# A graph layer and a routed expert layer on one core: the adjacency read through GpSimd's queue with the cast in the transfer

## What is computed

```
deg = max((adj != 0).sum(-1), 1)
# layer 1, on n = layernorm(x)
a_norm = rsqrt(deg) * (adj + eye) * rsqrt(deg)
x = x + relu((a_norm @ n + n) @ W + b)
# layer 2, on xf = layernorm(x)
probs = softmax(xf @ Wr + br);  top 2, weights divided by their sum
y = sum over experts e of combine[:, e] * (gelu(xf @ W1[e] + b1[e]) @ W2[e] + b2[e])
x = x + xf + y
```

## Time and profile before

| | us |
|---|---|
| median of 3 runs | 747.54 (747.32 to 748.49) |
| the profiled execution, its own time | 748.18 |
| the profiled execution, its span | 746.5 |
| mean granted TensorE clock | 0.951 of full speed |

### The profile page before, as it was taken

How to read it: one execution, slowest core, us unless ns; L and a number is a source line. 1 busy time by engine, 2 the same in 40 slices (tenths; PEclk the granted TensorE clock), 3 DMA queues, 4 the chain that set the end, 5 groups by cost and what they waited for, 6 DMA issues and landing times.

```text
span 746.5 us, 17744 instructions
## 1 busy us (share of the span) xinstructions
PE 603.4 (81%) x4798; PEld 462.1 (62%) x4799; DVE 472.2 (63%) x1366; ACT 344.5 (46%) x568; POOL 316.9 (42%) x296
## 2 busy tenths in 40 slices
PE   0049988887888989888887258999999999999994
PEld 0038866776666767677666225666666777777773
DVE  4966776676666767667666525766666565655562
ACT  2746656556464665655654113434343223322331
POOL 3631434344343443533425572454443444444444
PEclk9999999999999999999999558999999999999998
DMA  9548999999999999999984434565674444344320
GB/s 295 186 141 223 268 238 246 240 240 234 235 236 236 239 247 239 235 239 248 241 205 145 183 124 107 114 157 123 130 167 72 76 77 82 61 68 77 66 53 0
DMA packets 65915, 126.76 MB, mean 170 GB/s; under 512 B 9547, under 2 KB 40559, under 8 KB 65360
## 3 DMA queue, kind: packets, MB, share of 16 engines
q1 hardware_dynamic: 40240, 72.27, 37.8%
q10 hardware_dynamic: 10368, 35.66, 19.1%
q0 software_dynamic: 15264, 18.31, 13.9%
HBM read 103.71 MB, written 25.83 MB: 174 GB/s over the span
## 4 chain that ended last, share of the span: by engine, by line
DMA 39%; PE 26%; issue 13%; POOL 9%; DVE 6%; ACT 4%; POOLq 1%; ACTq 1%; SPq 1%; DVEq 0%
DMA rows<-feat,posi 23%; DMA out_dram<-orows,at_xg 9%; PE bank L536 9%; PE bank L559 8%; DMA abuf<-in_adj_dram 4%; POOL rows L1219 3%; PE bank L544 3%; ACT feat L635 2%; DMA wall<-in_x_dram 2%; PE bank L516 2%; POOL orows L1202 2%; POOL rows L1237 2%; PE bank L479 1%; PE bank L481 1%; DVE wall L826 1%
## 5 line engine op out<-in xcount | busy, mean ns | idle before, releaser
L479 PE MATMUL bank<-wall,at_xg 128*128 128x257 f16 x1024 | 244.7, 280 | 0.0
L481 PE MATMUL bank<-wall,at_xg 128*128 128x256 f16 x1024 | 244.4, 279 | 0.0
L1252 POOL DMA_INDIRECT out_dram<-orows,at_xg x79 | 127.5, 1614 | 164.5 <-DMA out_dram<-orows,at_xg 105.0
L601 ACT ACTIVATE a<-abuf 128x1024 f16<-128x1024 f32 x128 | 134.7, 1052 | 93.1 <-DMA abuf<-in_adj_dram 61.6
L744 ACT ACTIVATE a<-a 128x512 f32<-128x512 f32 x79 | 49.8, 630 | 184.7 <-DVE a L1072 184.7
L536 PE MATMUL bank<-wall,feat 128*128 x474 | 118.6, 387 | 10.3 <-issue 8.6
L479 PEld LDWEIGHTS bank<-wall,at_xg 128*128 128x128 f16 x1024 | 105.7, 103 | 14.7
L1078 DVE SCALAR_TENSOR_TENSOR wg<-bank,xseT 128x512 f16<-128x512 f32 x79 | 54.6, 692 | 92.1 <-ACT xseT L750 92.1
L1206 POOL TENSOR_TENSOR feat<-xf,feat 128x512 f16<-128x512 f32 x32 | 37.0, 1156 | 178.4 <-ACT feat L635 178.4
L816 DVE STREAM_TRANSPOSE at_xg<-a 128x512 int32<-128x512 int32 x128 | 90.6, 709 | 34.1 <-ACT a L601 24.7
L481 PEld LDWEIGHTS bank<-wall,at_xg 128*128 128x128 f16 x1024 | 102.5, 100 | 14.7
(11 more groups left out here) (152 smaller groups left out, 796.8 us busy)
## 6 DMA issues: line engine op xcount, KB each, us to landing
abuf<-in_adj_dram SPq DMA_DIRECT2D x64, 512.0 KB, 8.8
abuf<-in_adj_dram ACTq DMA_DIRECT2D x64, 512.0 KB, 12.3
wst<-in_L_ffn_W_dram SPq DMA_DIRECT2D x32, 512.0 KB, 5.3
at_xg<-rows SPq DMA_DIRECT2D x79, 136.0 KB, 2.4
out_dram<-orows SPq DMA_DIRECT2D x32, 128.0 KB
abuf<-in_L_ffn_b_dram SPq DMA_DIRECT2D x4, 1024.0 KB, 10.1
wall<-in_x_dram SPq DMA_DIRECT2D x8, 256.0 KB, 12.9
wall<-in_x_dram ACTq DMA_DIRECT2D x8, 256.0 KB, 13.2
```

The costliest lines, as they stand in the source:

```text
L479: both = [lambda: pe.matmul(ps_acc[odd][:, 0:D + 1], w, xh[:, j, 0:D + 1], start=j == 0, stop=j == T - 1), lambda: pe.matmul(ps_acc[odd][: ...
L481: lambda: pe.matmul(ps_acc[odd][:, 0:D], w, xl[:, j, :], start=False, stop=False)]
L601: act.activation(a16[:, c % 2, :].rearrange("p (a w) -> p a w", a=Q), arrived[:, k % 2, :, c * w:(c + 1) * w], ACT.Copy).then_inc(ev("cast ...
L1252: L.indirect_dma_start(out, bass.IndirectOffsetOnAxis(ap=info[r][:, 0:1].bitcast(U32), axis=0), orow[r], None, bounds_check=N - 1, oob_is_ ...
```

## The change

The adjacency's four DMAs per tile are issued by POOL, all four, and their destination is float16: `abuf` now holds four tiles of float16 in the bytes in which it held two of float32 (`AB = 4`), with one semaphore each. `cast`, its semaphore and `a16` are gone; DVE transposes straight out of `abuf`, and waits there for the tile's DMAs. SP and ACT issue no adjacency DMAs. The first three tiles are issued in POOL's prologue, between its steps on x; from then on POOL's step t begins with the four DMAs of tile t+3 (`more_adj`), ahead of `rstd1`; they wait until all chunks of tile t-1, which lay in the same buffer, are transposed.

The base is made by ACT alone: base = x1 * (rstd/2048 + 1) - mean * rstd/2048, with the two factors per token made by two small DVE instructions in front of `norm_x1` (`bs`). POOL's `make_base` is gone. At the very end of the phase `pads_before`, which lies in `xf`, waits for the last `low_part`.

The diff, cut:

```diff
 JC = CW // P
-CAST = 3
+AB = 4
 DEPTH = 3
...
 
-    abuf = sb("abuf", [P, 2 * Q * CW], F32)
-    arrived = abuf[:, :].rearrange("p (k a w) -> p k a w", k=2, a=Q)
-    b1all = abuf[:, :]
-    a16 = sb("a16", [P, 2, CW], F16)
+    abuf = sb("abuf", [P, AB * Q * CW], F16)
+    arrived = abuf[:, :].rearrange("p (k a w) -> p k a w", k=AB, a=Q)
+    b1all = abuf[:, :].bitcast(F32)
+    hgs = sb("hgs", [P, 2, H], F32)
     at_xg = sb("at_xg", [P, 2 * U * RW], F16)
...
     wst = sb("wst", [P, 2, DC * H], F32)
-    hg = [a16[:, k, :].bitcast(F32) for k in range(2)]
+    hg = [hgs[:, k, :] for k in range(2)]
     feat = sb("feat", [P, 2, TOPK, RW], F32)
...
     vr = sb("vr", [P, 2], F32)
+    bs = sb("bs", [P, 2], F32)
     lg = sb("lg", [P, E], F32)
...
     x_in = [sem(f"x_in{c}") for c in range(XC)]
-    a_in = [sem(f"a_in{k}") for k in range(2)]
+    a_in = [sem(f"a_in{k}") for k in range(AB)]
     w_in = [sem(f"w_in{k}") for k in range(2)]
...
 
-        eng.dma_start(arrived[b * PQ:(b + 1) * PQ, k % 2, :, :],
+        eng.dma_start(arrived[b * PQ:(b + 1) * PQ, k % AB, :, :],
                       adj_v[bass.ds(pair(i, k), 1), k % 2, b, :, :, :].rearrange("n i a c -> i (n a) c"))\
-           .then_inc(a_in[k % 2], 16)
+           .then_inc(a_in[k % AB], 16)
 
...
                 load_x(sp, c, b)
-            if c in (0, 2):
-                for b in QUEUE[0]:
-                    load_adj(sp, 0, c // 2, b)
         for dst, src in consts[0:2]:
...
         def load_b1():
-            sp.wait_ge(ev("cast"), T * CH)
+            sp.wait_ge(ev("at_made"), T * CH)
             b1_v = b1.rearrange("(c e) h -> c (e h)", c=CH).unsqueeze(1)
...
                 store_base(i, k - 3)
-            if is_(t, lambda t: t + 2 < T):
-                sp.wait_ge(ev("cast"), t * CH + CH)
-                for b in QUEUE[0]:
-                    load_adj(sp, i, k + 2, b)
             if isinstance(t, int) and t == T:
...
     def _(act):
-        def cast(i, k, c):
-
-            n = tile(i, k) * CH + c
-            act.wait_ge(a_in[k % 2], pair(i, k) * 16 * Q + 16 * Q)
-            if is_(n, lambda n: n >= 2):
-                act.wait_ge(ev("at_made"), n - 1)
-            w = CW // CH
-            act.activation(a16[:, c % 2, :].rearrange("p (a w) -> p a w", a=Q),
-                           arrived[:, k % 2, :, c * w:(c + 1) * w], ACT.Copy).then_inc(ev("cast"), 1)
-
         def cut_high_weights(i, which):
...
                 act.wait_ge(ev("b2_in"), 16)
-            act.activation(base[k % 2], xf[:, :], ACT.Copy, scale=1.0 / SX).then_inc(ev("base_scaled"), 1)
+            after(act, "base_scale", r)
+            after(act, "base_shift", r)
+            act.activation(base[k % 2], x1, ACT.Identity, scale=bs[:, 0:1], bias=bs[:, 1:2]).then_inc(ev("base_made"), 1)
 
...
                 load_x(act, c, b)
-            if c in (0, 2):
-                for b in QUEUE[1]:
-                    load_adj(act, 0, c // 2, b)
 
-        def more_adj(i, k):
-            act.wait_ge(ev("cast"), tile(i, k) * CH - CH)
-            for b in QUEUE[1]:
-                load_adj(act, i, k, b)
-
-        cast(0, 0, 0)
-        scale_x(0)
-        cast(0, 0, 1)
-        scale_x(1)
-        cast(0, 0, 2)
-        scale_x(2)
-        cast(0, 0, 3)
-        more_adj(0, 2)
-        scale_x(3)
+        for c in range(XC):
+            scale_x(c)
 
...
             for g in range(G):
-                if g % 2 == 0:
-                    k2, c2 = chunk(k, g // 2, CAST)
-                    if is_(tile(i, k2), lambda t2: t2 < T and (t2, c2) != (0, 3)):
-                        cast(i, k2, c2)
                 if g == 1 and has_v:
                     exps(v)
-                if g == 1 and is_(t, lambda t: 1 <= t < T - 2):
-                    more_adj(i, k + 2)
                 if g == 3 and has_s:
...
             n = tile(i, k) * CH + c
-            after(V, "cast", n)
+            V.wait_ge(a_in[k % AB], (tile(i, k) - k % AB) * (16 * Q // AB) + 16 * Q)
             if is_(n, lambda n: n >= CH):
...
             V.transpose(at[:, c, :].bitcast(I32).rearrange("p (n a i) -> p a n i", a=Q, i=PQ),
-                        a16[:, c % 2, :].bitcast(I32).rearrange("p (a n q) -> p a n q", a=Q, q=PQ))\
+                        arrived[:, k % AB, :, c * CW // CH:(c + 1) * CW // CH].bitcast(I32)
+                        .rearrange("p a (n q) -> p a n q", q=PQ))\
              .then_inc(ev("at_made"), 1)
...
                 after(V, "low_made", s - 1)
-                after(V, "base_scaled", s - 1)
+                after(V, "base_made", s - 1)
+            V.tensor_scalar(bs[:, 0:1], vr[:, 1:2], 1.0 / SX, 1.0, ALU.mult, ALU.add).then_inc(ev("base_scale"), 1)
+            V.tensor_scalar(bs[:, 1:2], mv[:, 0:1], vr[:, 1:2], -1.0 / SX, ALU.mult, ALU.mult).then_inc(ev("base_shift"), 1)
             V.tensor_scalar(xf[:, :], x1, mv[:, 0:1], vr[:, 1:2], ALU.subtract, ALU.mult)\
...
         after(V, "table_T", 0)
+        after(V, "low_made", T - 1)
         V.tensor_scalar(pads_before, ps_R[0:1, 2 * P:3 * P], 16.0, None, ALU.max).then_inc(ev("pads_table"), 1)
...
 
+        for b in range(Q):
+            load_adj(L, 0, 0, b)
         rstd0(0)
         rstd0(1)
+        for b in range(Q):
+            load_adj(L, 0, 1, b)
         low0(0)
...
         L.dma_start(rows[E * CAP:PLACES, :], pad[:, :]).then_inc(ev("padded"), 16)
+        for b in range(Q):
+            load_adj(L, 0, 2, b)
         low0(2)
...
 
+        def more_adj(i, k):
+            t = tile(i, k)
+            if is_(t, lambda t: t >= AB):
+                L.wait_ge(ev("at_made"), t * CH - (AB - 1) * CH)
+            for b in range(Q):
+                load_adj(L, i, k, b)
+
         def rstd1(s):
...
 
-        def make_base(i, k):
-            after(L, "base_scaled", tile(i, k))
-            L.tensor_tensor(base[k % 2], base[k % 2], x1, ALU.add).then_inc(ev("base_made"), 1)
-
         def low_part(s, odd):
...
             r, v = t - 2, t - 3
+            if is_(t, lambda t: t + AB - 1 < T):
+                more_adj(i, k + AB - 1)
             if is_(r, lambda r: 0 <= r < T):
...
                 low_part(r, odd)
-                make_base(i, k - 2)
             if is_(v, lambda v: 0 <= v < T):
```

## The result

The changed kernel takes 706.55 us, the median of 4 runs (704.46 to 707.11), against 747.85 (747.32 to 748.49, 4 runs) for the kernel before. The ratio is 0.944, with a 95% interval of 0.942 to 0.946. That is 5.6% less; 739 was forecast, inside a range of 695 to 795. The sign and the range held, the size did not: the gain is 41 us where 9 were forecast. The profiled execution took 704.46 us, its span 702.5.

A forecast was written before the change was run, and what follows sets the result against it. The prediction took POOL's serial step, P = 6.17 + 1.24 + 4I = 11.2 us with I = 0.95, as the new bound. Time = 748.2 + 4 + 26P + 16.3 - 321.2 = 738.5, forecast as 739 us, range 695 to 795.

The forecast's parts named there:

- the rival of cheap issues: POOL's DMA issues take 0.32 to 0.89 us, so PE may become the bound: 691 to 733 us, chance 0.24.
- the chain over POOL: POOL's serial step, from four issues to two row writes, becomes the new bound at 11.2 us: 733 to 747 us, chance 0.33.
- A loop over POOL and the row writes just as long: Kernel before: high_part, POOL's row writes and their landing (7.4 us) form a loop as long as the transfers.
- the transfer's rate: Adjacency loads with the cast in flight: 9 to 10 us a tile likely for all traffic, against 11.8 before.
- slow casts: Rival: the cast in flight lowers the transfers' rate, above 12.5 us a tile: 775 us and up, chance 0.15.
- unchanged transfers: Rival: transfers stay at 14.7 GB/s per engine, P = 11.8 us: 748 to 757 us, chance 0.10.
- dearer issues: Rival: each POOL issue costs more, from 1.05 us, delaying xf, high_part and low_part: 750 to 802 us, chance 0.16.
- the term I: POOL's time to issue one adjacency DMA, four a step ahead of its power: taken as 0.95 us.
- The front: Start of POOL's step, four issues with their gaps ahead of the power: 4 x 0.95 + 4 x 0.31, 5.0 us.
- P: Length of POOL's step in the graph phase, 6.17 + 1.24 + 4I: 11.2 us, counted for 26 steps.
- The rest of the chain: POOL's step without the issues and their gaps: power, DVE's factors and xf, high_part to first write, two writes: 6.17 us.
- The prologue: Before the steps: tile 0 lands near 20 to 22 us, delaying DVE's statistics; PE's first matmul 4 us later, bounds 0 and 9.

The follow-up runs named there:

- four powers: The changed kernel with four more small POOL power instructions in every step, between the four DMA issues and POOL's own power: 742.93 us, ratio 0.993.
- with two: The changed kernel with two more small POOL power instructions in every step, between the four DMA issues and POOL's own power: 718.87 us, ratio 0.960.
- the prologue's two edits: The changed kernel with DVE transposing tile 0's first chunk after x's statistics and POOL issuing tile 2 after its second low0: 698.09 us, ratio 0.931.

## Why the prediction was right in its parts and wrong in its size

The sign and the range held, the range because it took in the rival of cheap issues. The new bound that the prediction named, the chain over POOL, is not the bound of the changed kernel; PE is, with short waits for DVE.

**Right: the bound before.** Full queues were the bound, shown by the halved bytes (696). "A loop over POOL and the row writes just as long" was too much: shortened alone it gave 3 us, and with half the bytes its waits went.

**Right: what the casts on ACT are worth.** Nothing by themselves: with all of them in place, and half the bytes, a step takes 9.66 us.

**Right: the transfer's rate.** I took 19.6 GB/s per engine from the first tiles with x, measured is 20. That the two agree is in part luck: the 19.6 were float32 loads into both halves of the partitions at once, and nothing in that row told what a cast would do. The whole of the traffic then needed less than the 9.6 us forecast: share 0.86 of 9.79 us is 8.4 us a step. The rivals with slow casts or unchanged transfers are out, and so is that of dearer issues: the slowest of the 128 took 0.778 us.

**Right: the waits that go.** Those for the adjacency and for the rows' landing are gone from the profile, and the two-buffer run shows that the first needs loads issued further ahead than one step, as the deeper buffers allow.

**Wrong: the term I, POOL's time for an issue, and the gap beside it.** The step that failed was "For I the nearest row is POOL's one plain DMA, ... 0.895 us" with "I take I = 0.95" and "four issues with a gap of 0.31". Measured: 0.57 a piece back to back, 0.589 as a mean, no gap. The front is 2.3 us where 5.0 was in the sum. Two choices made this. The first: the one instance was POOL's first DMA of the program. In the changed kernel the same write of pad comes after eight others:

```profile
L1156 POOL DMA_DIRECT2D rows<-pad x1: 631/631/631, 42.5 to 42.5; - x1
...
L248 POOL DMA_DIRECT2D abuf<-in_adj_dram x128: 542/577/778, 6.5 to 327.7; - x128
```

The pad's write took 0.895 in the earlier trace rows and takes 0.631 here, and the slowest of the 128 loads, 0.778, is again the first. The second choice: the surcharge and the gap were read from the indirect writes, which are another kind of instruction. They still show both (1.07 us and 0.30 to 1.31 idle before); the plain loads show neither. The rows were few, and I treated the one instance as the middle of a range from 0.32 to 1.56 instead of a likely high value.

**What the other terms did.** With I at 0.57 and no gap the prediction's own sum gives P = 6.17 + 2.28 = 8.45 us, under PE's 9.3, that is its rival "issues are cheap, PE is the bound", at 691 us. The measured 704.5 differs from it by three things: step 3 comes 7.1 us later, not 4 (+3.1); the 28 steps take 273.5 us and not 260.4 (+13.1); the time after them is 3.4 shorter. The middle one is 0.5 us a step: PE's own work is 9.33 us, just what was said, and the 0.46 of idle time are nearly all waits for DVE (L416, 8.1 us in 24 steps, and L409, 2.7 in 5, together 0.45 a step). The five waits at L409, about 0.55 each, come with the return of the loop: every fourth step takes 10.3 us, the others 9.6. DVE is the busiest engine behind PE, at 84%. Its stall beside low_part is part of the 84; what the stall costs a step was not isolated.

**The rest of the chain came out 0.8 us long, and one gap in it had been hidden.** In the round with four powers above, all but the front takes 11.26 - 4.31 = 6.95 us, where the sum had 6.17. The two writes were 0.33 shorter (2.48 for 2.81). From the start of high_part to the first write it takes 3.17 us in the changed kernel (202.25 to 205.42), where 2.71 - 0.73 = 1.98 was said. After low_part POOL stands idle for 1.31 us before its first write. What it waits for is DVE. The write needs places and weights that DVE makes in a few small instructions; now they fall beside low_part, the conversion among them stalls until low_part ends, and the last of them ends at 204.39. The write begins 1.03 us later, and so it is in 23 of the 24 tiles between 100 and 340 us (the other took 1.36). In the kernel with only the base moved, DVE had ended 1.6 us or more before the write in 17 of 20 tiles, and there the gap was 0.17 us. So the 0.73 us of make_base do come out of the chain where DVE is early. In the changed kernel DVE is late, and they do not. With 6.95, which is taken from the run with four powers, the sum gives 6.95 + 3.33 = 10.3 with two (measured 10.32), and 6.95 + 2.28 = 9.2 for the changed kernel, which is the slack of about 0.55 us under its 9.79.

**The prologue.** Forecast: PE's first product 4 us later, bounds 0 and 9; measured 6.4. The mechanism was the one named. Tile 0 landed at 21.31, forecast 20 to 22, and the statistics of x's second chunk began at 21.95 instead of 16.02:

```profile
21.31 0.71 DVE L781 STREAM_TRANSPOSE at_xg<-abuf 128x512 int32<-128x512 int32 x1 [10.46 <-DMA abuf<-in_adj_dram]
```

Those 5.9 us alone, for which 4 had been put in, explain most of the size. The rest is where POOL's two low0 fall beside DVE. The first holds a small instruction of the third chunk's statistics for 4.66 us where it was 3.40. The second stood beside `scale_some` before, and stands beside DVE's low_x now. The six instructions of `scale_some`, before and after, then low_x and the low0 beside it:

```profile
35.10 5.94 DVE L826 TENSOR_SCALAR wall<-wall,mean,rstd 128x256 f32<-128x256 f32 x6 [0.27 <-POOL rstd L1166]
```
```profile
42.23 2.03 DVE L792 TENSOR_SCALAR wall<-wall,mean,rstd 128x256 f32<-128x256 f32 x6 [0.27 <-POOL rstd L1135]
...
47.00 5.40 DVE L768 TENSOR_TENSOR wall<-wall 128x2048 f16<-128x2048 f32 x1
```
```profile
45.46 4.79 POOL L1143 TENSOR_TENSOR wall<-wall 128x2048 f16<-128x2048 f32 x1
```

Low_x took 2.24 us in its second half before. So 3.9 us are saved at `scale_some` and 3.2 lost at low_x, and 5.9 + 1.3 - 3.9 + 3.2 comes near the 6.4 measured. The prediction had no term for any of these stalls; that they nearly cancel is luck. In the kernel with the prologue's two edits `scale_some` takes 5.75 us again and low_x 2.24.

**Two slips in the rivals' sums.** By its own formula, 447.3 + 26P, an issue of 1.2 us gives 764.5 us, not 760, and P = 11.8 gives 754, where up to 757 is written. Neither touches the forecast.

**What was said to show it.** A spacing of 11.2 us, POOL busy 80% (63 measured), DVE waiting for POOL's power: none of these. The power that no longer waits for DVE, the waits for DMAs that go and a DMA share under 0.95 came as said. The prediction had also said what would prove it wrong, "the plain DMAs under 0.7", and that is what came.

## What to carry to other kernels

Price an instruction that a change adds from repeated rows of its own kind; where the trace has only one, ask whether it is the first of its engine, and give the cheap case the weight that the missing rows leave it. Where float32 is loaded only to be cast, a cast in flight can do more than save the casts: it sped up reading by a third here, from 14.7 to 20 GB/s per engine. Halving the bytes of each kernel told in one run whether transfers were the bound at all. A faster transfer needs an early enough issue: with two buffers and an issue one step ahead the same change gave nothing.
